# Attention layer with a macaron FFN: GpSimd's last indirect store of a step goes from ahead of the small-block inversion to between its two parts

## The reference

```python
def step(S, ch):                       # one chunk of C = 64 tokens, for 2 sequences x 4 heads
    Q, K, V, bt = ch
    Kb = K * bt
    Vb = V * bt
    A = jnp.eye(C) + jnp.tril(jnp.einsum('bhcd,bhed->bhce', Kb, K), -1)
    T = solve_triangular(A, jnp.broadcast_to(I32, A.shape), lower=True)
    W = T @ Kb
    U = T @ Vb
    St = S.swapaxes(-1, -2)
    mid = U - W @ St
    O = Q @ St + jnp.einsum('bhcd,bhed->bhce', Q, K) * M @ mid
    S_new = S + mid.swapaxes(-1, -2) @ K
    return (S_new, O)

x = x + 0.5 * ffn(layernorm(x))        # 8 experts, top 2 per token
x = x + attention(layernorm(x))        # x is [2, 4096, 256]
x = x + 0.5 * ffn(layernorm(x))        # same weights
```

## Time and profile before

| | us |
|---|---|
| median of 3 runs | 1590.0 |
| lowest, highest | 1588.88, 1592.53 |
| the profiled execution: its span | 1602.7 |
| first FFN, up to about | 450 |
| attention, from about 450 to about | 1294 |
| GpSimd busy over the span | 889.9 |

### The profile page before, as it was taken

How to read it: one execution, slowest core, us unless ns; L and a number is a source line. 1 busy time by engine, 2 the same in 40 slices (tenths; PEclk the granted TensorE clock), 3 DMA queues, 4 the chain that set the end, 5 groups by cost and what they waited for, 6 DMA issues and landing times. The chain is left out here.

```text
span 1602.7 us, 47314 instructions
## 1 busy us (share of the span) xinstructions
PE 1349.0 (84%) x17084; PEld 1208.4 (75%) x17084; DVE 1099.0 (69%) x2928; ACT 882.4 (55%) x1836; POOL 889.9 (56%) x1579
## 2 busy tenths in 40 slices
PE   7758888888557999999999999999997558878886
PEld 7757877877546888888888888878886457778775
DVE  7774454454376788989898998988984565543553
ACT  4424553455245777776676676676773335534552
POOL 3562455254536556657766676766757324562545
PEclk8978998998878999999999999999997779999998
DMA  8437663764101222222222222222223576537651
GB/s 249 161 115 228 215 202 122 266 212 159 57 22 25 42 51 47 52 60 71 74 63 68 67 70 64 75 70 65 71 56 81 169 222 221 192 152 246 207 179 60
DMA packets 218577, 193.42 MB, mean 121 GB/s; under 512 B 105188, under 2 KB 182250, under 8 KB 218352
## 3 DMA queue, kind: packets, MB, share of 16 engines
q1 hardware_dynamic: 184800, 114.06, 26.1%
q0 software_dynamic: 24576, 67.94, 11.5%
q10 hardware_dynamic: 8976, 8.40, 1.7%
HBM read 102.63 MB, written 94.01 MB: 123 GB/s over the span
## 5 line engine op out<-in xcount | busy, mean ns | idle before, releaser
L1734 DVE SCALAR_TENSOR_TENSOR raw_w<-attn_raw,taps,raw_w 128x256 f32<-128x256 f32 x576 | 240.9, 486 | 4.5 <-ACT raw_w L2143 4.5
L525 PE MATMUL ffn_both<-ws,ffn_xhi 128*128 x1152 | 211.7, 297 | 8.7 <-DVE ffn_xlo L743 3.8
L525 PEld LDWEIGHTS ffn_both<-ws,ffn_xhi 128*128 128x128 f32 x1152 | 170.9, 198 | 17.6 <-issue 17.2
L2421 POOL TENSOR_TENSOR attn_inv<-attn_inv,attn_term 64x14 f32<-64x14 f32 (+6 forms) x448 | 134.0, 299 | 35.1
L548 PE MATMUL ffn_yb<-ws,ffn_hhi 128*128 x576 | 132.0, 308 | 23.2 <-issue 14.7
L748 DVE TENSOR_TENSOR ffn_hid<-ffn_both,ffn_sil 128x512 f32<-128x512 f32 x72 | 49.6, 689 | 142.0 <-ACT ffn_sil L870 94.5
L2418 POOL TENSOR_TENSOR attn_term<-attn_small,attn_inv 64x14 f32<-64x14 f32 (+6 forms) x448 | 126.3, 282 | 32.6
L1334 PE MATMUL attn_fr<-attn_xhi,wqkv 128*128 128x256 f32 x768 | 139.3, 290 | 5.1 <-ACT attn_bth L2150 2.4
L870 ACT ACTIVATE ffn_sil<-ffn_both 128x512 f32<-128x512 f32 x72 | 42.8, 595 | 154.3 <-remote 108.0
L2460 POOL TENSOR_TENSOR attn_factors<-attn_squared,attn_powers 128x10 f32<-128x10 f32 x28 | 55.1, 1969 | 129.1 <-DVE attn_squared L1832 129.1
L548 PEld LDWEIGHTS ffn_yb<-ws,ffn_hhi 128*128 128x128 f32 x576 | 101.7, 204 | 32.8 <-issue 32.4
(11 more groups left out here) (342 smaller groups left out, 3904.0 us busy)
## 6 DMA issues: line engine op xcount, KB each, us to landing
ffn_xb<-second_rows SPq DMA_DIRECT2D x48, 259.0 KB
ffn_more_rows<-second_rows SPq DMA_DIRECT2D x48, 259.0 KB
raw_w<-second_rows SPq DMA_DIRECT2D x40, 259.0 KB
ffn_more_rows<-first_rows SPq DMA_DIRECT2D x64, 131.0 KB, 2.1
attn_xin<-x_after_first ACTq DMA_DIRECT2D x32, 256.0 KB, 2.7
attn_xres<-x_after_first SPq DMA_DIRECT2D x32, 256.0 KB
x_after_attention<-attn_xres SPq DMA_DIRECT2D x32, 256.0 KB
attn_xg<-x_after_attention SPq DMA_DIRECT2D x32, 256.0 KB, 3.1
```

The source lines that it names most:

```text
L525: last = pe.matmul(hp[:, j, :], (xhi, xlo)[b][:, k % 2, q, j * P:(j + 1) * P], ws[:, bass.ds(experts[j], 1), a, q].rearrange("p o d -> p ( ...
L1734: dve.scalar_tensor_tensor(acc[:, j, r], raw[:, j, r, :, tap:tap + P], taps[:, j, r, tap:tap + 1], acc[:, j, r], ALU.mult, ALU.add)\
L2421: pool.tensor_tensor(v[:, j + 1:, 0:j], v[:, j + 1:, 0:j], term[:, 0:k, 0:j], ALU.subtract)\
```

## The change

In GpSimd's `body`, the two parts of `invert_blocks` are taken apart. The last single store of a step (tile 2, 4 or 7) is called after the first part. The stores of the groups 6 and 7 and the earlier ones of a step keep their places.

```diff
                 if s and more:
                     both_factors(s, f)
-                if v and v[1] == 2 and (0 < v[0] < LAST):
-                    gate_scatter((v[0] - 1, 1), 4, 5)
-                if v and v[1] == 1 and (0 < v[0] < LAST):
-                    gate_scatter((v[0] - 1, 0), 2, 3)
                 if v and v[1] == 3 and (v[0] == LAST - 1):
                     gate_scatter(v, 0, 2)
                 if s and (not more):
                     out_factor(s)
                 if v and v[1] == 3 and (v[0] == LAST - 1):
                     gate_scatter(v, 2, GB)
+                if g:
+                    invert_blocks(g, 1, SB // 2 - 2)
+                if v and v[1] == 2 and (0 < v[0] < LAST):
+                    gate_scatter((v[0] - 1, 1), 4, 5)
+                if v and v[1] == 1 and (0 < v[0] < LAST):
+                    gate_scatter((v[0] - 1, 0), 2, 3)
                 if v and v[1] == (2 if v[0] == LAST - 1 else 3) and (0 < v[0] < LAST):
                     gate_scatter((v[0] - 1, 2), 7, 8)
                 if g:
-                    invert_blocks(g, 1, SB // 2 - 2)
                     invert_blocks(g, SB // 2 - 2, SB - 1)
```

## The result

| | before | changed |
|---|---|---|
| median of 6 runs, us | 1588.47 | 1603.32 |
| lowest, highest | 1584.58, 1592.53 | 1597.82, 1611.01 |
| span of the profiled execution | 1602.7 | 1600.3 |

The ratio is 1.0084, with an interval from 1.0056 to 1.0112: 13 us slower by the ratio (the medians lie 14.9 us apart), where 5.3 were forecast. The range ended at 1601.0.

The account below looks back on a forecast made before the run. Attention's loop was taken as bound by a chain, not one busy engine. Block 31's inversion 1.3, SP's queue 2.8 and `turn16` 1.2 summed to 5.3 us on 1590.0, giving 1595.3 us; range 1589.5 to 1601.

Parts of the forecast that it names:

- The delay of the inversion: On GpSimd, the store inside makes the inversion end 1.3 us later in 16 steps, bounds 1.0 and 1.6.
- GpSimd's own next work: `remainder_scaled` after the inversion has 2.0 us before PE's `mids` need it, against 1.3 of delay: cost 0.
- Rival 2: GpSimd's lateness reaches `mids` if the store costs over 1.6 us: 1605 us, chance 0.06.
- The chain of DVE, PE and ACT: Attention's loop is bound by a chain; DVE idles 1.0 us a step for PE's first products, behind `mids` and `turn16`.
- SP's ring and `turn16`: SP's queue delays spread, take and `lower_blocks`, 2.8 us; late placing delays PE's `turn16`, 1.2 us.
- The last inversion: Block 31's inversion has no projection beside it to hide the delay, so 1.3 us goes straight on the path.
- The contention rule: Beside DVE's convolution a store is a better neighbour than an inversion; takes contention off about 1 us of it.
- rival 3: Faster: DVE's convolutions relieved by the store beside them, 0.15 us a step, 1589.0 us, chance 0.08.

Follow-up runs that it names:

- late inversion: Kernel before plus an unused power between the inversion's two parts, all stores in their old places: 1.0081; 1.0084 where the kernel before takes about 1454 us.
- c = 2 alone: Only the c = 2 store (tile 4) moved into the inversion's middle, the other two as in the kernel before: ratio 1.0061.
- late stores: Kernel before plus an unused power behind `remainder_scaled` in ten c = 2 and c = 3 steps: 1.0089 with before at 1602.0 us, 0.9997 with before at 1453 us.

## Why the prediction was wrong

- **The delay of the inversion** was sized 1.3 us with bounds 1.0 and 1.6. It is 1.58, at the upper bound: the store 1.07, 0.38 ahead of it and not 0.20, and the 0.5 us operation, whose return was foretold. The reason given for it was wrong: block 31's inversion has no store right ahead of it now either, and its like took 0.25. What it goes with is DVE's convolution, in the 20 traces (blocks 10 to 31 of each). Where the operation starts 0.04 to 0.08 us behind the convolution's first one, it takes 0.50 to 0.54 us (341 inversions); where it starts ahead of it or with it (79), or where there is no convolution (block 31's, 20), 0.24 to 0.25. In block 19's step it started 0.11 us ahead of it before, and starts 0.07 behind it now. The diagonal stands 0.06 us behind `lower_blocks`, with 1.39 us of idle ahead.
- **GpSimd's own next work: here the step failed.** "That leaves 2.0 us for a delay of 1.3 ... So 0" asks only whether `mids` waits for `remainder_scaled`. It does not, as forecast: 941.90 plus half of 1.20 against 942.77. But the stores behind `remainder_scaled` are late as well, and the prediction does not count them at all. On the chips where the kernel takes 1588 us and more they hold back PE's news, and 1.6 us later they lie on `mids` and `turn16`: the steps concerned lose 7.5 + 2.6 = 10 of the 13.5 us, of which at most 1.3 can be the ring's waits at `turn16`. Rival 2 named `mids`, with another reason (a wait for GpSimd's data) and a wrong threshold; its 1605 is near by chance.
- **The chain of DVE, PE and ACT** was read rightly as the bound: "whatever holds PE at either of the two is paid in full". 8.7 of the 13.5 us stand in the first row. The 1.77 us of idle at 975.32 before, against 1.0 on average, was there to be asked about.
- **SP's ring and `turn16`**, 2.8 + 1.2 us, were the right places, and the size is right for one of the traces. In that of the result it is mainly one lump, 3.7 us with the slower clock behind it. Where nothing is withheld the ring is the whole loss: in the changed kernel 2.9 us of waits at `lower_blocks` and 2.1 at `turn16`, 4.7 us over the twenty steps, but 5 to 10 us in the four traces with a late inversion there (472.3 against 477.0, 478.1, 480.1 and 481.9) and 6 to 12 by the ratios. In such a case the term was too small. SP's wait for DVE at the spread fell from 15.7 us in 24 steps to 7.3 in 8.
- **The last inversion**, 1.3 us, cost nothing in this profile. Before, `turn16` came 1236.00 - 1220.29 = 15.71 us behind the diagonal; now it is 15.78. The inversion ended 1.5 us later, but the placing took 2.68 us to PE, not 3.43, and the collection 2.04 to the placing, not 2.74. These intervals scatter by half as much as the term; one execution is no measure of it.
- **The contention rule** of the Trainium skill, SBUF — State Buffer, section Who interferes with whom, holds in its small way: the 64x54 operation went back from 0.37 to 0.30 us, the 0.5 us operation above fits it too, and the eight operations of the convolution take 3.36 us with the store beside them, 3.39 before. That relief of DVE is 0.03 us a step; rival 3 needed 0.15. What it says of who can disturb whom did not help with the large effect: PE and ACT were not slowed, they were told late.
- **PE's clock** adds to the loss. In three of the five c = 3 steps of the changed kernel (blocks 17, 21 and 25), and once behind DVE's wait at block 14, the granted clock falls to half behind the longer pause. Before, it did so nowhere in the twenty steps. One window of it (us, then busy time of each engine, the clock, DMA share, GB/s), and the step's like before:

```profile
972.00:975.00 3.00, 3.00 (x68) 1.81 (x48) 1.98 (x6) 1.71 (x5) 1.24 (x1) 0.50 0.82 198
```

```profile
976.00:979.00 3.00, 3.00 (x62) 2.59 (x62) 2.92 (x10) 2.49 (x7) 2.18 (x2) 1.00 0.73 190
```

PE is at 1.2 GHz for these 3 us, where it was at 2.4. The steps tell the two parts apart. In the four kernels whose stores fall on `mids` in the c = 3 steps (the changed one, c = 2 alone, late inversion, late stores), the seven such steps without a stretch at half the clock are 1.0 to 1.2 us longer than before, the 13 with one 1.4 to 2.1. So the withheld news costs some 1.1 us there by itself, and the clock up to 1 us more. Why the clock falls in some of these steps and not in others, the traces don't tell.

## What to carry to other kernels

When work on one engine is moved, list everything queued behind it on that engine as later too, and ask of each item what it will now run beside, not only who waits for its data. An idle time that is longer than its like in the neighbouring steps, and ends when some third engine's instruction ends, is a disturbance to be understood before anything is moved near it. And a verdict that depends on such an effect should be tried on more than one chip: an experiment that shows nothing may have met one where the effect does not exist.

## What the hardware showed

- While GpSimd issued an indirect store of 128 rows (1.0 to 1.2 us), the semaphore events of PE's finished matmuls came up to 1.3 us late, mostly shortly behind the store's end, and up to 2.2 us with two stores in a row; 43 of 49 under a store were held, none of 569 elsewhere. For DVE and ACT the traces don't show it: their events near the stores are partly missing and can't be matched one to one.
- On three chips nothing of the kind was seen for PE, and the same kernel took 1453 to 1455 us, some 9% less. The twenty steps are 9 us shorter there (472.3 with the late stores, 481.3 before) and the first FFN some 70 us (first diagonal at 397 to 406 us, 468 to 480 on the others). The two FFNs have 352 such stores (64 of line 925, 288 of line 934), and the same count gives 76 of 115 ends of PE under a store late in the first FFN of the trace of before, 78 of 103 in the second (away from stores 10 of 76 and 2 of 52), and on a quick chip (late stores) 0 of 164 and 0 of 80. So news is withheld there too; that this is what makes the FFNs slower was not tested.
- The collection of the inverses, behind which the placing is issued 2.02 us later in most steps, held it up for 3.2 to 5.1 us now and then (four times in the kernel with the store moved in c = 3 alone). The cause is open.
